# Staging the int32 up-weights of a gated MLP through Vector casts, and two edits to weight-load ordering, in a two-layer transformer kernel

## What is computed

```python
# layer 0: attention with rotary embedding, 16 query heads, 4 key/value heads;
# ffn: 16 routed experts (width 512, top 4 of 16 by a router) and 2 shared ones
# layer 1: causal attention with 16 heads of 64; ffn with int32 weights:
SCALE = 1.0 / 127.0                      # w_gate, w_up: [3072, 1024] int32
wg, wu, wd = (w.astype(x.dtype) * SCALE for w in (w_gate, w_up, w_down))
gate = jnp.einsum('bsd,hd->bsh', x, wg)
up   = jnp.einsum('bsd,hd->bsh', x, wu)
h    = jax.nn.silu(gate) * up
return jnp.einsum('bsh,dh->bsd', h, wd)
```

## Time and profile before

| | us |
|---|---|
| median of the 2 runs shown | 4789.41 |
| the two runs | 4761.94 and 4816.88 |
| the profiled execution's own time | 4771.61 |
| its span on the slowest core (core 7) | 4770.1 |
| spans of the 8 cores | 4740.1 to 4770.1 |

### The profile page before, as it was taken

The page is one execution under the profiler, slowest core; times in us unless marked ns, Lnnn a source line. Parts: engine busy times, 40 slices in busy tenths (PEclk is TensorE's granted clock), DMA queues, the critical chain, the costliest instruction groups (busy, mean ns, idle before and its releaser), DMA issues.

```text
span 4770.1 us, 44313 instructions; the slowest of 8 cores (4740.1 to 4770.1 us)
## 1 busy us (share of the span) xinstructions
PE 3590.2 (75%) x14712; PEld 1435.7 (30%) x14712; DVE 1285.9 (27%) x2076; ACT 1329.3 (28%) x1573; POOL 282.4 (6%) x522
## 2 busy tenths in 40 slices
PE   2246666799999999995777777752899976577776
PEld 0012222344434444442222222211344432122222
DVE  3333330033023103302222222225211112544333
ACT  1100000011011101101666666621111100456663
POOL 1000000000000000000000000001111100000000
PEclk8568888899999999998999999975999999899998
DMA  3247777834434334431011211134444421122212
GB/s 71 70 130 199 206 198 189 211 133 146 146 133 141 142 141 142 150 141 27 12 18 36 44 38 33 36 88 112 71 75 73 74 48 27 22 56 51 45 36 69
DMA packets 139086, 450.92 MB, mean 95 GB/s; under 512 B 15568, under 2 KB 15728, under 8 KB 122480
## 3 DMA queue, kind: packets, MB, share of 16 engines
q0 software_dynamic: 73632, 218.42, 22.0%
q1 hardware_dynamic: 65232, 229.67, 14.0%
HBM read 490.23 MB, written 73.40 MB: 118 GB/s over the span
## 4 chain that ended last, share of the span: by engine, by line
PE 54%; DMA 16%; DVE 14%; ACT 9%; issue 5%; DVEq 1%; SPq 0%; ACTq 0%; POOL 0%; POOLq 0%
PE pst L747 8%; ACT a16t L1543 8%; PE pst L761 7%; PE pst L864 4%; PE pb L864 4%; DMA a32t<-l_u 4%; PE pb L1481 3%; PE pb L1005 3%; DMA a16t<-s_g 3%; PE pst L941 3%; PE pst L952 3%; PE pst L1507 3%; PE pst L1512 3%; PE pb L1486 2%; PE pst L1395 2%
## 5 line engine op out<-in xcount | busy, mean ns | idle before, releaser
L1543 ACT ACTIVATE a16t<-pst 128x1024 bf16<-128x1024 f32 x832 | 852.2, 1024 | 449.7 <-PE pst L1512 377.9
L747 PE MATMUL pst<-xn_sb,a16t 128*128 128x512 bf16 x2304 | 590.4, 403 | 195.8 <-DVE a16t L695 167.6
L761 PE MATMUL pst<-xn_sb,a16t 128*128 128x512 bf16 x2304 | 558.9, 386 | 0.0
L774 ACT ACTIVATE a32t<-pst 128x512 f32<-128x512 f32 x288 | 172.0, 597 | 1107.6 <-PE pst L747 1107.6
L782 DVE TENSOR_TENSOR a32t<-a32t,pst 128x512 f32<-128x512 f32 x256 | 175.9, 687 | 1119.1 <-PE pst L761 1113.2
L1481 PE MATMUL pb<-a16t 128*65 128x512 bf16 x832 | 331.3, 398 | 179.1 <-DVE a16t L1560 92.9
L1507 PE MATMUL pst<-a16t 128*128 128x512 bf16 x832 | 338.3, 407 | 163.2 <-DVE a16t L1440 103.5
L747 PEld LDWEIGHTS pst<-xn_sb,a16t 128*128 128x128 bf16 x2304 | 225.5, 102 | 510.0 <-issue 288.1
L1512 PE MATMUL pst<-a16t 128*128 128x512 bf16 x832 | 339.1, 408 | 0.0
L1486 PE MATMUL pb<-a16t 128*65 128x512 bf16 x832 | 328.9, 395 | 0.0
L761 PEld LDWEIGHTS pst<-xn_sb,a16t 128*128 128x128 bf16 x2304 | 230.6, 100 | 290.2 <-issue 32.6
(11 more groups left out here) (156 smaller groups left out, 2788.2 us busy)
## 6 DMA issues: line engine op xcount, KB each, us to landing
a16t<-s_g POOLq DMA_DIRECT2D x108, 512.0 KB, 5.0
a16t<-s_u SPq DMA_DIRECT2D x108, 512.0 KB, 4.1
a32t<-l_u SPq DMA_DIRECT2D x32, 1024.0 KB, 10.0
a16t<-s_d SPq DMA_DIRECT2D x27, 1024.0 KB, 5.9
a16t<-s_d POOLq DMA_DIRECT2D x27, 1024.0 KB, 5.4
s_g<-a16t SPq DMA_DIRECT2D x36, 512.0 KB, 6.9
s_u<-a16t SPq DMA_DIRECT2D x36, 512.0 KB, 8.0
s_d<-a16t SPq DMA_DIRECT2D x18, 1024.0 KB, 7.1
```

The costliest lines, as they stand in the source:

```text
L747: li = t.matmul(pb[gp_][:, :], a16t[:, o_gb[wp] + hc * 256 + ici * 128: o_gb[wp] + hc * 256 + ici * 128 + 128], xn_sb[:, hc * T + tc * TC: ...
L761: li = t.matmul(pb[up_][:, :], a16t[:, o_ub[wp] + hc * 256 + ici * 128: o_ub[wp] + hc * 256 + ici * 128 + 128], xn_sb[:, hc * T + tc * TC: ...
L1543: return s.activation(a16t[:, o_pt[kp4]:o_pt[kp4] + 2 * TC], pst[kp][:, 0:1024], AF.Exp, scale=0.125)
```

## The change

Three edits.

1. In `phase_B0` the down-weight loads of chunk 0 no longer depend on `hlast[max(0, e - 4)]`.
2. In `phase_B1` the up weights no longer come by a converting load on G. They are loaded raw (int32) on Q into two new staging buffers of 1024 words in `a32t`, each load depending on the cast that emptied its buffer two blocks before, and a new VectorE operation, `f_ucast`, casts the staged block to bfloat16. It depends on the raw load and on the last product of block `ic - 2`. It is added between the loads and the matmuls of its block. The gate weights stay as they were.
3. In `phase_C` `preload_group` is gone. The Wo load of a group is added to G when the group is started.

```diff
@@ phase_B0
                     if tc == 0:
-                        dld.append(hlast[max(0, e - 4)])
                         opldd = P.add("G", f_ldd, deps=dld,
                                       sem=sW[2 + wp], name=f"B0ldd{tc}.{e}")
@@ phase_B1
             o_silu = [a32.alloc(TC) for _ in range(2)]
+            o_st1 = [a32.alloc(1024) for _ in range(2)]
...
-                    def f_ldu(q, usrc=usrc, wp=wp):
+                    def f_ldur(q, usrc=usrc, wp=wp):
                         if q is None:
                             return 1
                         return q.dma_start(
-                            out=a16t[:, o_ub[wp]:o_ub[wp] + 1024], in_=usrc)
+                            out=a32t[:, o_st1[wp]:o_st1[wp] + 1024].bitcast(I32),
+                            in_=usrc)
...
-                    opldu = P.add("G", f_ldu, deps=[bp] + fen, sem=sW[wp],
-                                  name=f"B1ldu{sc}.{ic}")
+                    opldur = P.add("Q", f_ldur,
+                                   deps=[prev.get(("st1", wp))] + fen,
+                                   sem=sWu[wp], name=f"B1ldur{sc}.{ic}")
+
+                    def f_ucast(v, wp=wp):
+                        with nc.allow_low_precision(reason="i32 weight -> bf16"):
+                            return v.tensor_copy(
+                                a16t[:, o_ub[wp]:o_ub[wp] + 1024],
+                                a32t[:, o_st1[wp]:o_st1[wp] + 1024].bitcast(I32))
+                    opldu = P.add("V", f_ucast, deps=[opldur, bp],
+                                  name=f"B1ucast{sc}.{ic}")
+                    prev[("st1", wp)] = opldu
@@ phase_C
-            preg = [None]
-
-            def preload_group():
-                if preg[0] is None and pend:
+            def start_group():
+                if curg[0] is None and pend:
                     g = pend.pop(0)
                     g[0]()
-                    preg[0] = g
-
-            def start_group():
-                if curg[0] is None:
-                    if preg[0] is None and pend:
-                        g = pend.pop(0)
-                        g[0]()
-                        preg[0] = g
-                    if preg[0] is not None:
-                        g = preg[0]
-                        preg[0] = None
-                        curg[0] = g
-                        curg[1] = list(g[1:-1])
+                    curg[0] = g
+                    curg[1] = list(g[1:-1])
...
-                        if kc == nkc // 2:
-                            preload_group()
```

## The result

| | before | after |
|---|---|---|
| profiled execution (us) | 4771.61 | 4847.53 |
| span of its slowest core | 4770.1 (core 7) | 4845.9 (core 6) |
| mean span of the 8 cores | 4754.2 | 4832.0 |
| median of all runs | 4804.34 (10 runs) | 4851.16 (11 runs) |

The ratio after to before is 1.0163, with a 95% interval of 1.0136 to 1.019: slower, by less than 2%. The profiled executions differ by 75.9 us. The mean spans, which don't depend on which core happens to be last, differ by 77.8.

What follows compares the result with a forecast made beforehand. The prediction took TensorE as the bound: passes +40.6 and +35.8, start +2.4, sum +78.8 us, giving 4852 for the profiled execution; about half of the shown runs' 18 us offset made it 4860, range 4825 to 4910.

Steps and rivals of the forecast that it cites:

- What bounds the stretch: Layer 1's two gate-and-up passes: TensorE bounds them, so every idle microsecond put in lengthens the kernel by one.
- Edits 1 and 3 at nothing: Layer 0's down loads and the attention's Wo and Wq loads: dropped dependency and later Wo load each change the time by 0.
- The idle stretch: At each of 46 block boundaries in layer 1's passes, TensorE is empty for product, cast and hand-overs: 1.82 us.
- The passes: Layer 1's two gate-and-up passes: 214.0 us against 173.4 (+40.6) and 212.3 against 176.5 (+35.8), with a block period of 8.89.
- the clock rival: TensorE's clock falls at layer 1's block boundaries: 46 falls of about 1.68 us, 77 us, giving 4930; chance 0.07.
- The gross and the net: Layer 1's passes: the +40.6 and +35.8 us already include the saved waits for loads, 14 us in all.
- The start: Start of layer 1's gate-and-up phase: raw load, cast and hand-overs delay the first gate matmul to 3352.5 from 3350.1, +2.4 us.
- The total: Whole kernel: sum +78.8 us on core 7, 4852 for the profiled execution, 4860 for a fresh run.
- The slow cast: Layer 1's int32 cast runs at one column a cycle: 24 us more, 4877, 2.2% slower; chance 0.10.
- The gate load: Layer 1's gate load, issued under the cast, becomes late; a third of them by 1 us gives 4868; chance 0.04.
- Not slower: The cast runs in VectorE's idle 2.77 us ahead of a product, so no boundary idles: 4760; chance 0.03.

## Why the prediction was right

**What bounds the stretch.** Confirmed. PE's busy time in the passes grew by 2 us and their length by some 40; 46 x 1.81 us of idle time came in, one for one.

**Edits 1 and 3 at nothing.** Confirmed by the run with them alone: ratio 0.9987, with an interval of 0.35% to either side, and both attentions within 1.4 us on the mean (1192.9 and 895.1). The places in POOL's order came out as worked out: the down loads directly behind the last gate load, Wo unmoved, Wq 21 us earlier.

**The idle stretch.** Forecast 0.11 + 0.69 + 0.19 + 0.69 + 0.14 = 1.82; measured 0.10 + 0.69 + 0.17 + 0.69 + 0.15 = 1.80, which the trace, before rounding, has as 1.81. The hand-over to the cast was 0.02 shorter. The price of the int32 cast was the one open bound, 0.686 or 1.219. The profile page's line group has it:

```profile
L939 DVE CAST a16t<-a32t 128x1024 bf16<-128x1024 int32 x48 | 33.3, 694 | 8.8 <-DVE a16t L980 8.4 <-DMA a32t<-l_u 0.3
```

694 ns for 1024 columns: the SBUF rate of 0.529 ns a column holds for an int32 source. The Trainium skill, Vector Engine (DVE) Microarchitecture Reference, section 5.1, puts no condition on the data type for two results a cycle from one source in SBUF; the trace agrees, with this 694 ns.

**The passes.** Forecast 214.0 and 212.3; the means over the cores are 214.2 and 214.0. The period of 8.89 measured 8.87 to 8.88. The second pass fits on core 6 alone, the one whose window stands above (212.6). The other seven took 214.2 us each. At one boundary of this pass, on every core, the cast begins 0.52 us after the product and not 0.17, and the idle stretch is 2.16 us (on two cores 2.37 and 2.54). Behind it the clock stayed up on core 6 and fell on the other seven. On core 0:

```profile
3665.43 0.69 DVE L939 CAST a16t<-a32t 128x1024 bf16<-128x1024 int32 x1 [0.52 <-DVE a16t L980]
...
3666.27 2.99 PE L952 MATMUL pst<-xn_sb,a16t 128*128 128x512 bf16 x8 [2.16 <-DVE a16t L939]
```

So the clock rival came true once on seven of the eight cores, for some 1.5 us each. Why that cast is late no run shows.

**The gross and the net.** This term was a little off. For the phase the prediction had +76.4 on core 7, and core 7 shows 515.4 before and 594.7 after, +79.3; the fall of the clock is about half of the difference. The mean over the cores is +82.1, because the other cores had waited less for loads before: on the mean 10.0 us were to be won (511.7 to 501.7), on core 7 13.7. The prediction saw this for core 1 (2.4 us less to win back) and took it for that core alone. The gross cost is 92.1 us (593.8 less 501.7), or 2.00 a boundary: the idle 1.81, 0.16 by which the modelled end of eight matmuls (1.89) lies behind the start of the next eight (1.73), and 0.03 for the one fall.

**The start.** Forecast +2.4. In the changed kernel the first gates begin at 3346.87, 1.2 us after the last normalising product has ended (3345.69); with a hand-over of about 0.2 they could have begun 1.0 us earlier. The landing was as forecast, 5.7 us from issue (3340.34) to the cast (3346.03). What was off is the issue: it lay 6.5 us ahead of the gate matmuls on this core, and the prediction had taken the 4.4 us of the earlier trace rows. The mean stretch ahead of the phase did not grow at all (1194.3 to 1191.9).

**The total.** The sum of 78.8 us stands against 77.8 in the mean spans and 75.9 in the profiled times: by the means, the phase brought 5.7 us more than forecast (82.1 for 76.4), the stretch ahead of it 4.8 less (-2.4 for +2.4), and the other phases -1.6. That the sum came within 1 us of the means is partly luck, since these errors cancel. The predicted 4860 includes 8 us for the spread of the two runs shown, and lies above the range of 4843 to 4853. The profiled sum of 4852 stands against 4847.53; that it meets the median of 4851.16 in the table is luck as well.

**The rivals.** The slow cast is excluded by the 694 ns. The gate load is not late: no gate matmul waits for it. Its issue took 0.53 us at the median and at most 0.80, and in the timeline above the one at 3374.40, which began under a cast, took 0.53 like the others, where the prediction had taken 0.99. It isn't a matter of course: with half a cast more in front, the same issue took 0.94 us at the median, and still no gate matmul waited for its load. "Not slower" would have needed the cast in front of a product. That is just what the run with the cast moved ahead does, and it gives the 4760 of that rival, within its spread (4754 to 4770 in six executions). The mechanism and the price were right, the place in VectorE's order decides. The clock rival had its price nearly right: 1.68 us a fall, where its own rows give 3.33 - 1.89 = 1.44 and the runs 1.5 to 1.6. Its condition was too far off: see below.

## What to carry to other kernels

Before moving a conversion to an idle engine, write down that engine's order around the block boundary. If the new operation stands behind the last product of block n and in front of the first matmul of block n + 1, its length plus every hand-over is idle time, however low the engine's busy share; put it behind an earlier operation of block n, where its input has already landed. Here that made it free, 92 us for a few moved lines. In layer 0 the input had not landed, and the same move gave only a part. The same holds for a queue: a load that stands behind a write-back waits for whatever the write-back waits for, and in layer 0 of this kernel that alone was 89 us of 480, more than the whole change cost. And ask what the loads can give at most: a third buffer without any cast reached the same 502 us.

## What the runs showed of the hardware

TensorE's granted clock stayed at the 2.4 GHz level after every idle stretch of 1.81 us between stretches of 7 us of matmuls, some 45 on each of the eight cores. In the same kernel it stayed there after two stretches of 2.02 us, and fell after seven of the eight of 2.16 to 2.54 us. In the kernels with a longer cast it was at the 1.2 GHz level after about half of the stretches of 2.31 us, two fifths of those of 2.57, and nearly all of those of 3.34. A fall cost 1.5 to 1.6 us, in the eight matmuls behind the idle stretch or, with three casts, in part in the next eight. I had taken 2.85 us in layer 0, where it fell only sometimes, as the nearest case for trouble; but the row of 2.19 us in layer 1's attention, followed by the low level, was the better hint. How often the clock fell did not grow steadily with the idle time, and no run here says why.

VectorE's cast of 128 x 1024 from int32 to bfloat16, from SBUF to SBUF, took 694 ns, on the line through the casts from float32 (415 ns for 512 columns, 1227 for 2048).
